# Cross-attention queries from split fp32r parts, the low parts kept over x, and a new order of the units around them

## The chip, the cores and the metric

One Trainium2 chip, one of its cores. The time is that of one execution on the device in microseconds (us). TensorE (PE), VectorE (DVE), ScalarE (ACT), GpSimd (POOL) and SyncE (SP, which here only starts DMAs) each run an instruction stream of their own, in order, and wait for each other through semaphores.

## The reference

A decoder layer over x and ctx of 8 batches x 512 rows x 256 columns, all fp32:

```python
x = layernorm(x + linear_attention(x))        # state memory, M=128, decay 0.99
x = layernorm(x + cross_attention(x, ctx))    # 16 heads of 16: q = x @ w_q.T + b_q; k, v from ctx
x = layernorm(x + self_attention(x) + moe(x)) # 16 heads; 8 experts 256x256, the two best by gate
```

The change is in `q = x @ w_q.T` of the cross attention, and in what lies around it.

## The kernel before

**Phases and slots.** Each batch n has a cross-attention phase C n and a self-attention phase S n. They run in the order C0, C1, S0, C2, S1, ..., C7, S6, S7. A phase has 16 slots, so slot s runs from 0 to 255, and each slot has two halves, an even and an odd one (t = 2s and 2s+1). In each half PE computes two score tiles `sc`, two tiles `mx` for the row maxima of a group six slots ahead, and in even halves also the product of probabilities and values `op`. ACT takes the exponential of `sc` (line 801), DVE the maxima of `mx` (line 990, three PSUM banks, one `mx` tile each).

**Units.** All other work of PE is cut into units: for a batch q1, k1, v1, s0, s1, s23, o1, y01, y23 (linear attention), x0 and x1 (transposes of the normalised rows x1 into x1T, 4 of 128x128 each), qc0 and qc1 (cross q), kc0, kc1, cv0, cv1 (cross k, v), hT, cy, x2T, k3c, q3c, v3, gate, be and moe0 to moe15, and for each group of four slots `shift` (a transpose of the maxima) and `heads` (4 transposes of oT). The tables LIN_* (relative to the start of phase C n), MID_* and MOE_* say in which half slot a unit stands. From slot 0 on, PE runs the units of both halves of a slot in its odd half, after `sc` and `mx`, in the order of the tables (line 725). For n of 3 to 7 the table LIN holds; phase C n starts at slot 32n-16.

**Banks.** Units write two PSUM banks `ms` in turn. A unit waits until the unit two before it has been taken out (lines 538 to 539):

```python
if u >= 2:
    wait_unit_out(pe, *ORDER[u - 2])
```

ACT and DVE take out the units of half t-1 when they come to half t. On ACT that is after its exponential of half t, on DVE after its two maxima of half t; a few kinds (EARLY_OUT) go ahead of the maxima, and only in even halves. So in a slot with `shift` (even half) DVE copies shift_r (line 954) behind the two maxima of the odd half.

**Cross q before.** Line 764 copies x0 and x1 on ACT into x1T (fp32); line 576 multiplies with the fp32 weight w_wq, two products of 512 columns in a unit. A product in fp32 stands in the trace as two instructions. The others of this kind (kc, cv, k3c, q3c, v3, moe) already use parts: a value is the sum of a high part rounded to fp32r (by ACT) and a low part, the rest (by DVE or POOL), and hi*hi + lo*hi + hi*lo is computed, six instructions in a unit (project_parts, line 502).

**Memory of x.** x_s holds x of a batch, then x plus the linear attention, and from n = 2 on also the staged context (load_ctx, ctx_high on ACT, ctx_low on POOL, line 1217). load_x brings the next batch's x, after ln_out[0] and ctx_low. x_bias (POOL, line 1213) adds a bias to it.

Of the kernel before, what the change touches and what calls it, by code (L numbers as in the profile page):

```python
# [12 lines left out]
P = 128  # L13
# [6 lines left out]
E = 8  # L20
# [28 lines left out]
             "x_bias": (-21, 0), "x1_bias": (-17, 0), "load_xT": (-21, 1), "load_x": (-12, 0)}  # L49
# [15 lines left out]
       "x_bias": (-27, 0), "x1_bias": (7, 0), "load_xT": (-31, 0), "load_x": (-11, 1), "load_ctx": (-17, 1),  # L65
# [17 lines left out]
MOE_FIRST = [(24, 1), (25, 1), (28, 0), (29, 1), (30, 1), (31, 0), (31, 1), (32, 1), (33, 0), (33, 1), (35, 1), (36, 1), (37, 0),  # L83
# [164 lines left out]
STAGED = ("we", "wqkv3", "be", "wk2", "wv2")  # L248
# [8 lines left out]
def decoder(nc, x, xT, ctxT, w, out):  # L257
    with ExitStack() as ctx:
        def sb(name, shape, dt=F32):
            return ctx.enter_context(nc.sbuf_tensor(name, shape, dt))  # L260
# [20 lines left out]
        combT = sb("combT", [TERMS * E, T])[:]  # L281
        gateT = sb("gateT", [P, P])[:]
# [3 lines left out]
        x2T_part = (sb("x2T_hi", [P, DC, T]), sb("x2T_lo", [P, DC, T]))  # L286
        part = {n: sb(n + "_parts", [P, 2, T]) for n in "qk"}
# [27 lines left out]
        comb3 = sb("comb3", [P, TB, TERMS * E])  # L315
# [35 lines left out]
        zeros, xb_out, x1b_out, x2_high, x2_low = sem("zeros"), sem("xb_out"), sem("x1b_out"), sem("x2_high"), sem("x2_low")  # L351
# [4 lines left out]
        LATE = tuple(n for n in w if n not in FIRST + EARLY + STAGED)  # L356
        block = ctx.enter_context(nc.Block())
# [33 lines left out]
        def _(sp):  # L391
            def load(name, n):
                if name == "load_xT":
                    if n >= 1:
                        wait_unit(sp, "k1", n - 1)
                        wait_unit(sp, "v1", n - 1)
                    sp.dma_start(xT_s[:], xT[n:n + 1].rearrange("o (c p) t -> p (o c) t", p=P)).then_inc(xT_in, 16)
                elif name == "load_x":
                    if n >= 1:
                        sp.wait_ge(ln_out[0], TB * n)  # L400
                    if n >= 3:
                        sp.wait_ge(ctx_low, DC * n)
# [75 lines left out]
        def _(pe):  # L478
# [23 lines left out]
            def project_parts(dst, wt, src, cols):  # L502

                for m, (i, j) in enumerate(((0, 0), (1, 0), (0, 1))):
                    for c in range(DC):
                        last = mm(dst, wt[j][:, c, cols].bitcast(F32R), src[i][:, c, :].bitcast(F32R),
                                  m == 0 and c == 0, m == 2 and c == DC - 1)
                return last

            def project_part_rows(bank, width, src, wt, cols, blocks):  # L510

                for b, t in enumerate(blocks):
                    for m, (i, j) in enumerate(((0, 0), (1, 0), (0, 1))):
                        for c in range(DC):
                            last = mm(bank[:, b * width:(b + 1) * width], src[i][:, c, t * P:(t + 1) * P].bitcast(F32R),
# [18 lines left out]
            def unit(task, n):  # L534
# [31 lines left out]
                elif task in ("kc0", "kc1"):  # L566
# [4 lines left out]
                    last = project_parts(bank, w2_part["wk2"], ctxT_part, slice(c * P, c * P + P))  # L571
                elif task in ("qc0", "qc1"):
# [3 lines left out]
                    last = project(bank, W["wq2"], x1T, slice(c * P, c * P + P))  # L576
                elif task in ("cv0", "cv1"):
# [4 lines left out]
                    last = project_part_rows(bank, D, ctxT_part, w2_part["wv2"], slice(0, D), (2 * h, 2 * h + 1))  # L582
# [19 lines left out]
                elif task in ("k3c0", "k3c1", "q3c0", "q3c1"):  # L602
# [6 lines left out]
                    last = project_parts(bank, w3_part, x2T_part, slice(at, at + P))  # L609
                elif task in ("v3a", "v3b"):  # L610
# [5 lines left out]
                    last = project_part_rows(bank, D, x2T_part, w3_part, slice(2 * D, 3 * D), (2 * h, 2 * h + 1))  # L616
# [116 lines left out]
        def _(act):  # L733
# [16 lines left out]
            def take_out(task, n):  # L750
# [92 lines left out]
            for t in range(FIRST_HALF, LAST_HALF + 1):  # L843
# [6 lines left out]
                if t == lin_at("y01", 0):  # L850
# [3 lines left out]
                    nc.scalar.mul(W["wq2"][:], W["wq2"][:], HD ** -0.5).then_inc(scaled, 1)  # L854
# [38 lines left out]
        def _(dve):  # L893
# [17 lines left out]
            def take_out(task, n):  # L911
# [55 lines left out]
                elif task in ("x2T0", "x2T1"):  # L967
                    c = int(task[3])
                    dve.wait_ge(x2_high, DC * n + c + 1)
                    nc.vector.tensor_tensor(x2T_part[1][:, c, :].bitcast(F32R), bank, x2T_part[0][:, c, :],  # L970
                                            ALU.subtract).then_inc(x2_low, 1)
# [211 lines left out]
        def _(pool):  # L1183
# [140 lines left out]
```

## Time and profile before

| | before |
|---|---|
| median of 3 runs | 1255.2 us (1250.92 to 1255.43) |
| profiled execution, its time | 1252.54 us |
| its span | 1250.8 us |
| busy PE, DVE, ACT, POOL | 96%, 74%, 62%, 31% |

The span reaches from the first to the last instruction; 1.7 us of the execution lie around it. Busy PE counts overlapping instructions once; a matmul's recorded duration is longer than the distance to the next one's start, so lengths in PE are read from start to start. Slot 0 starts at 67.69 us. Half slots are given below as stretches from one `sc` to the next.

### The profile page before, as it was taken

The page shows a single profiled execution, that of the slowest core. Times are in us where ns is not written, and L with a number is a line of the kernel's source. Part 1 is how long each engine was busy: PE and PEld are TensorE (multiplying, and loading weights), DVE is VectorE, ACT ScalarE, POOL GpSimd, SP SyncE. Part 2 cuts the span into 40 slices and gives each one's busy share as a digit, 9 for nine tenths or more (in the row PEclk, how much of TensorE's full clock was granted, in tenths as well). Part 3 has the DMA queues.
Part 4 walks back from the last instruction along what each step waited for, and adds up shares of the span by engine and source line. Part 5 has one row for each costly group of instructions (what it writes and reads, how often), then busy time and mean ns, then how long its engine had stood idle before and what let it go on. Part 6 is the DMA issues. An engine that isn't in the chain of part 4 may idle for free.

```text
span 1250.8 us, 20663 instructions
## 1 busy us (share of the span) xinstructions
PE 1204.7 (96%) x6998; PEld 599.3 (48%) x6998; DVE 922.8 (74%) x1867; ACT 778.6 (62%) x1090; POOL 381.9 (31%) x485
## 2 busy tenths in 40 slices
PE   8799999999999999999999999999999999999998
PEld 4443444545545445454554454454544444554443
DVE  3687886677777787777877778777877788678772
ACT  2355567675576665765667656667657666666664
POOL 5510113311522134420523206221153204430261
PEclk9999999999999999999999999999999999999999
DMA  7422122122222122222122222222122211212200
GB/s 251 118 57 65 44 52 69 44 52 57 56 69 63 36 66 57 61 65 54 48 63 70 56 56 69 47 66 52 40 57 68 52 39 42 67 28 52 52 19 18
DMA packets 56446, 74.99 MB, mean 60 GB/s; under 512 B 14720, under 2 KB 26520, under 8 KB 56088
## 3 DMA queue, kind: packets, MB, share of 16 engines
q1 hardware_dynamic: 55192, 72.96, 23.4%
q8 instruction: 57, 0.93, 0.3%
q10 hardware_dynamic: 1152, 0.72, 0.2%
q14 instruction: 45, 0.37, 0.1%
HBM read 18.06 MB, written 4.19 MB: 18 GB/s over the span
## 4 chain that ended last, share of the span: by engine, by line
PE 80%; DVE 7%; ACT 6%; issue 4%; SPq 1%; DMA 1%; ACTq 0%; POOL 0%; DVEq 0%
PE ms L480 36%; PE op L480 15%; PE sc L480 15%; PE mx L480 9%; DVE maxes L990 3%; ACT probs L801 3%; PE ms L590 2%; PE ms L531 2%; ACT moe L794 1%; SPq L427 1%; PE ms L585 1%; DMA w_ident<-in_ident 1%; ACT k_parts L737 1%; DVE q_parts L900 0%; DVE heads L963 0%
## 5 line engine op out<-in xcount | busy, mean ns | idle before, releaser
L990 DVE TENSOR_REDUCE maxes<-mx 128x1 f32<-128x512 f32 x1024 | 657.5, 684 | 198.7 <-PE mx L480 196.9
L801 ACT ACTIVATE probs<-sc 128x1024 f32<-128x1024 f32 x512 | 525.0, 1025 | 369.1 <-PE sc L480 364.9
L1240 POOL TENSOR_TENSOR x<-x,moe 128x256 f32<-128x256 f32 x256 | 187.4, 732 | 646.3 <-ACT moe L794 624.7
L480 PE MATMUL op<-probs,v 128*32 128x512 f32 x2048 | 272.8, 605 | 0.4 <-ACT probs L801 0.3
L480 PE MATMUL sc<-qs,ks 50*128 50x512 f32 x1024 | 256.3, 497 | 13.8 <-ACT probs L801 12.8
L480 PEld LDWEIGHTS sc<-qs,ks 50*128 50x128 f32 x1024 | 95.3, 183 | 307.1 <-ACT probs L801 234.8
L480 PE MATMUL mx<-ks,qs 48*128 48x512 f32 x1024 | 209.5, 404 | 8.9 <-DVE maxes L990 6.7
L794 ACT ACTIVATE moe<-ms,comb 128x256 f32<-128x256 f32 x256 | 107.1, 473 | 20.1 <-PE ms L480 20.1
L480 PEld LDWEIGHTS mx<-ks,qs 48*128 48x128 f32 x1024 | 97.4, 187 | 22.4 <-DVE maxes L990 16.6
L480 PE MATMUL ms<-we_hi,x2T_hi 128*128 128x512 f32 x256 | 92.8, 443 | 3.2 <-DVE q_parts L900 1.0
L480 PEld LDWEIGHTS op<-probs,v 128*32 128x32 f32 x2048 | 40.3, 108 | 93.7 <-issue 92.0
L480 PE MATMUL ms<-we_hi,x2T_lo 128*128 128x512 f32 x256 | 80.5, 395 | 0.0
L480 PE MATMUL ms<-we_lo,x2T_hi 128*128 128x512 f32 x256 | 80.4, 395 | 0.0
L480 PEld LDWEIGHTS ms<-we_hi,x2T_hi 128*128 128x128 f32 x256 | 39.4, 188 | 34.8 <-issue 14.7
L480 PEld LDWEIGHTS ms<-we_lo,x2T_hi 128*128 128x128 f32 x256 | 48.0, 188 | 11.8
L480 PEld LDWEIGHTS ms<-we_hi,x2T_lo 128*128 128x128 f32 x256 | 48.1, 188 | 11.7
L590 PE MATMUL ms<-w_ident,oT 128*128 128x128 f32 x256 | 41.0, 283 | 2.4 <-DVE shift_r L954 1.6
L900 DVE SCALAR_TENSOR_TENSOR k_parts<-ms,w_bk,k_parts 128x512 fp32r<-128x512 f32 x32 | 24.0, 751 | 25.2 <-ACT k_parts L737 24.2
L1195 POOL TENSOR_SCALAR var<-mv 128x4 f32<-128x4 f32 x24 | 5.5, 230 | 113.9 <-DVE mv L1021 98.8
L736 ACT ACTIVATE oT<-op 128x512 f32<-128x512 f32 x64 | 38.0, 594 | 1.4 <-PE op L480 1.4
L590 PEld LDWEIGHTS ms<-w_ident,oT 128*128 128x128 f32 x256 | 28.2, 141 | 21.9 <-DVE shift_r L954 16.7
L737 ACT ACTIVATE k_parts<-ms,w_bk 128x512 fp32r<-128x512 f32 x32 | 22.0, 686 | 24.5 <-PE ms L480 18.0
(155 smaller groups left out, 1302.4 us busy)
## 6 DMA issues: line engine op xcount, KB each, us to landing
ks<-k_parts SPq DMA_DIRECT2D x384, 64.0 KB, 2.3
qs<-q_parts SPq DMA_DIRECT2D x381, 64.0 KB, 2.2
xT_s<-in_xT SPq DMA_DIRECT2D x8, 512.0 KB, 3.8
x_s<-in_x SPq DMA_DIRECT2D x8, 512.0 KB, 4.2
out<-x SPq DMA_DIRECT2D x7, 512.0 KB, 3.1
x_s<-in_ctxT SPq DMA_DIRECT2D x6, 512.0 KB, 5.1
qs<-shift_r SPq DMA_DIRECT2D x128, 8.0 KB
x<-in_ctxT SPq DMA_DIRECT2D x2, 512.0 KB, 6.3
```

The lines of the kernel that those rows point to most:

```text
L427: sp.dma_start(dst[at:at + HD, g % RING, :, :], part[name][src:src + 32, which[r], :]).then_inc(stack_in[name][g % 2], 16)
L480: return nc.tensor.matmul(dst, lhsT, rhs, start=first, stop=last, skip_group_check=True)
L531: last = nc.tensor.transpose(bank[:, t * P:(t + 1) * P], src[:, t, c * P:(c + 1) * P], ident[:])
L585: last = nc.tensor.transpose(bank[0:SHIFT * HG * TB, 0:P], shift_n[:, n % 2].rearrange("p s a m -> p (s a m)"), ident[:])
L590: last = nc.tensor.transpose(bank[:, t * P:t * P + P], oT[:, t * P:t * P + P], ident[:])
L736: return nc.scalar.activation(dst, src, ACT.Copy)
L737: return nc.scalar.activation(dst, src, ACT.Identity, bias=bias, scale=1.0)
L794: nc.scalar.activation(moe[:, k % 2, j * D:j * D + D], bank[:, j * D:j * D + D], ACT.Copy, scale=comb[:, t, e:e + 1]).then_inc(moe_out, 1)
L801: nc.scalar.activation(probs[:, (2 * s + h) % 3, :, :], sc[:], ACT.Exp).then_inc(exp_out, 1)
L900: nc.vector.scalar_tensor_tensor(out=part[name][:, 1, :].bitcast(F32R), in0=unit_bank((task, n)), scalar=bias[:, c:c + 1], in1=part[name][ ...
L990: nc.vector.tensor_reduce(maxes[:, g % 2, at:at + 1], mx[:, i % 3, :], AX_X, ALU.max).then_inc(max_out, 1)
L1240: nc.gpsimd.tensor_tensor(x2[:, n % 2, t, :], x2[:, n % 2, t, :], moe[:, k % 2, j * D:j * D + D], ALU.add).then_inc(acc, 1)
```

## The change

Units qc0 and qc1 use parts of x1T and of wq2. The high parts lie where x1T lay, the low parts of x0 and x1 lie in the memory of x_s; DVE makes them. So x of the next batch can be loaded only after qc1, and load_x moves (LIN: from slot -11 to -4). x0 and x1 can be taken out only when the context staged in x_s has been split, and x0, x1 and qc0 move (LIN: from -16, -15, -14 to -14, -14, -13). In batch 2 s1, s23, o1, y01 and y23 move earlier, and in batch 0 one moe unit (35, 1) moves to (32, 0), with the next ones in turn. wq2 is staged over x2T_lo, scaled and rounded by ACT, and its low part made by POOL. combT, gateT and comb3 (the experts' weights, transposed) lie over o1T.

```diff
-             "x_bias": (-21, 0), "x1_bias": (-17, 0), "load_xT": (-21, 1), "load_x": (-12, 0)}
+             "x_bias": (-21, 0), "x1_bias": (-17, 0), "load_xT": (-21, 1), "load_x": (-5, 0)}
...
-              "x_bias": (-4, 0), "x1_bias": (20, 1), "load_xT": (-4, 0), "load_x": (3, 0), "load_ctx": (-13, 0),
+              "x_bias": (-4, 0), "x1_bias": (20, 1), "load_xT": (-4, 0), "load_x": (11, 0), "load_ctx": (-13, 0),
...
-LIN_THIRD = {"q1": (-37, 1), "k1": (-36, 1), "v1": (-41, 1), "s0": (-35, 1), "s1": (-34, 1), "s23": (-33, 1),
-             "o1": (-32, 1), "y01": (-30, 0), "y23": (-29, 0), "x0": (-20, 0), "x1": (-19, 0), "x_bias": (-34, 0),
+LIN_THIRD = {"q1": (-37, 1), "k1": (-36, 1), "v1": (-41, 1), "s0": (-35, 1), "s1": (-34, 0), "s23": (-34, 1),
+             "o1": (-33, 1), "y01": (-32, 0), "y23": (-32, 1), "x_bias": (-35, 0),
...
-       "o1": (-23, 1), "y01": (-21, 0), "y23": (-20, 0), "x0": (-16, 0), "x1": (-15, 0), "qc0": (-14, 0),
+       "o1": (-23, 1), "y01": (-21, 0), "y23": (-20, 0), "x0": (-14, 0), "x1": (-14, 1), "qc0": (-13, 0),
...
-       "x_bias": (-27, 0), "x1_bias": (7, 0), "load_xT": (-31, 0), "load_x": (-11, 1), "load_ctx": (-17, 1),
+       "x_bias": (-27, 0), "x1_bias": (7, 0), "load_xT": (-31, 0), "load_x": (-4, 0), "load_ctx": (-17, 1),
...
-MOE_FIRST = [(24, 1), (25, 1), (28, 0), (29, 1), (30, 1), (31, 0), (31, 1), (32, 1), (33, 0), (33, 1), (35, 1), (36, 1), (37, 0),
+MOE_FIRST = [(24, 1), (25, 1), (28, 0), (29, 1), (30, 1), (31, 0), (31, 1), (32, 0), (32, 1), (33, 0), (33, 1), (36, 1), (37, 0),
...
+        combT = over("combT", [TERMS * E, T], "o1T", 4 * T)[:]
+        gateT = over("gateT", [P, P], "o1T", 4 * T)[:]
+        comb3 = over("comb3", [P, TB, TERMS * E], "o1T", 4 * T)
+        x1T_part = ([over(f"x1T_hi{c}", [P, T], "x1T", 4 * T * (DC - c)) for c in range(DC)],
+                    [over(f"x1T_lo{c}", [P, T], "x_s", 4 * T * (DC - c)) for c in range(DC)])
+        wq2_part = (sb("wq2_hi", [P, DC, D]), sb("wq2_lo", [P, DC, D]))
...
                     if n >= 1:
-                        sp.wait_ge(ln_out[0], TB * n)
-                    if n >= 3:
-                        sp.wait_ge(ctx_low, DC * n)
+                        wait_unit(sp, "qc1", n - 1)
...
-                    last = project(bank, W["wq2"], x1T, slice(c * P, c * P + P))
+                    if n == 0:
+                        pe.wait_ge(wq2_low, 1)
+                    last = project_parts(bank, wq2_part, x1T_part, slice(c * P, c * P + P))
...
-                elif task in ("x0", "x1"):
-                    wait_unit(act, task, n)
-                    copy(x1T[:, int(task[1]), :], bank).then_inc(done, 1)
...
+                elif task in TRANSPOSED:
+                    name, c = task[:-1], int(task[-1])
+                    if name == "x2T" and n == 0:
+                        act.wait_ge(wq2_low, 1)
                     wait_unit(act, task, n)
-                    copy(x2T_part[0][:, int(task[3]), :].bitcast(F32R), bank).then_inc(x2_high, 1)
+                    copy(rows_part[name][0][c][:].bitcast(F32R), bank).then_inc(rows_high[name], 1)
...
+                elif task in TRANSPOSED:
+                    name, c = task[:-1], int(task[-1])
+                    dve.wait_ge(rows_high[name], DC * n + c + 1)
+                    if name == "x" and n >= 2:
+                        dve.wait_ge(ctx_low, DC * (n + 1))
+                    nc.vector.tensor_tensor(rows_part[name][1][c][:].bitcast(F32R), bank, rows_part[name][0][c][:],
+                                            ALU.subtract).then_inc(rows_low[name], 1)
...
-                    nc.scalar.mul(W["wq2"][:], W["wq2"][:], HD ** -0.5).then_inc(scaled, 1)
+                    act.wait_ge(wq2_in, 16)
+                    nc.scalar.mul(wq2_stage, wq2_stage, HD ** -0.5).then_inc(scaled, 1)
+                    act.wait_ge(scaled, 3)
+                    copy(wq2_part[0][:].bitcast(F32R), wq2_stage).then_inc(wq2_high, 1)
...
                     pool.wait_ge(w_late, 16 * len(LATE))
+                    pool.wait_ge(wq2_high, 1)
+                    nc.gpsimd.tensor_tensor(wq2_part[1][:].bitcast(F32R), wq2_stage, wq2_part[0][:], ALU.subtract).then_inc(wq2_low, 1)
```

A unit x0 or x1 now counts as out when DVE has written its low part (rows_low).

## Rows read from the trace of the kernel before

**Rows 1.** The page: busy time, share of the span and instructions of each engine.

```profile
PE 1204.7 (96%) x6998; PEld 599.3 (48%) x6998; DVE 922.8 (74%) x1867; ACT 778.6 (62%) x1090; POOL 381.9 (31%) x485
```

**Rows 2.** Windows: stretch, length, busy (count) per engine, granted clock, DMA share, GB/s.

```profile
355.53:357.80 2.27, 2.27 (x16) 1.35 (x12) 2.24 (x5) 1.56 (x3) 1.46 (x2) 1.00 0.26 58
372.56:375.21 2.65, 2.65 (x18) 1.73 (x14) 2.13 (x5) 2.65 (x6) 1.43 (x2) 1.00 0.18 34
376.88:379.91 3.03, 3.03 (x17) 1.52 (x13) 2.15 (x5) 1.81 (x4) 2.32 (x4) 1.00 0.00 0
381.58:383.82 2.24, 2.24 (x14) 1.42 (x11) 2.21 (x6) 1.03 (x1) 0.00 (x0) 1.00 0.32 73
230.39:234.04 3.65, 3.65 (x21) 2.55 (x17) 2.54 (x6) 1.03 (x1) 0.00 (x0) 1.00 0.39 88
417.73:420.90 3.17, 3.17 (x16) 1.39 (x12) 2.96 (x6) 1.51 (x2) 0.00 (x0) 1.00 0.36 83
```

**Rows 3.** Groups of instructions by line and shape: count, busy us, mean ns of one.

```profile
L970 DVE TENSOR_TENSOR x2T_lo<-ms,x2T_hi 128x512 fp32r<-128x512 f32 x16 | 10.9, 687 | 2.0 <-ACT x2T_hi L736 1.3
...
L736 ACT ACTIVATE x1T<-ms 128x512 f32<-128x512 f32 x16 | 9.6, 604 | 1.3 <-PE ms L531 1.3
```

**Rows 4.** Timeline of PE, odd half of slot 66: start, length, instruction.

```profile
377.54 0.28 PE L585 MATMUL ms<-w_ident,shift_n 128*32 128x128 f32 x1
377.66 1.89 PE L480 MATMUL ms<-x1T,w_wq 128*128 128x512 f32 x4
379.38 0.60 PE L590 MATMUL ms<-w_ident,oT 128*128 128x128 f32 x4
```

**Rows 5.** Timelines of DVE and ACT in the same half.

```profile
376.28 2.65 DVE L990 TENSOR_REDUCE maxes<-mx 128x1 f32<-128x512 f32 x4
378.85 0.27 DVE L954 COPY shift_r<-ms 32x128 f32<-32x128 f32 x1
...
377.42 1.02 ACT L801 ACTIVATE probs<-sc 128x1024 f32<-128x1024 f32 x1
```

**Rows 6.** Timeline of PE in slot 30, odd half: a unit behind shift's bank.

```profile
204.73 0.50 PE L480 MATMUL sc<-qs,ks 50*128 50x512 f32 x2
...
207.03 0.73 PE L480 MATMUL ms<-we_hi,x2T_hi 128*128 128x512 f32 x2 [0.91 <-DVE shift_r L954]
```

**Rows 7.** Timelines of PE and DVE in slot 75, odd half from 417.73.

```profile
418.99 1.99 PE L480 MATMUL ms<-x1T,w_wq 128*128 128x512 f32 x4
...
418.51 0.42 DVE L963 TENSOR_TENSOR heads<-ms,rsum 128x256 f32<-128x256 f32 x1
```

**Rows 8.** Windows: slots 28 and 29, then halves of slots 32, 14, 15, 16, 57.

```profile
194.69:203.07 8.38, 7.78 (x47) 4.37 (x43) 6.25 (x10) 6.24 (x10) 2.78 (x3) 1.00 0.49 125
216.07:218.70 2.63, 2.33 (x14) 1.34 (x10) 1.67 (x3) 2.63 (x6) 1.41 (x2) 1.00 0.23 54
126.68:129.75 3.07, 2.37 (x15) 1.11 (x12) 2.89 (x6) 1.02 (x1) 0.00 (x0) 1.00 0.01 3
131.41:133.03 1.62, 1.59 (x12) 0.97 (x8) 1.59 (x5) 1.02 (x1) 0.00 (x0) 1.00 0.35 81
134.71:138.17 3.46, 3.46 (x21) 2.12 (x18) 1.94 (x4) 1.51 (x2) 0.00 (x0) 1.00 0.41 95
336.70:339.71 3.01, 3.01 (x16) 1.73 (x12) 2.03 (x5) 1.56 (x3) 1.45 (x2) 1.00 0.36 121
```

**Rows 9.** The page's DMA issues; timelines of SP, POOL and DVE at the start.

```profile
x_s<-in_x SPq DMA_DIRECT2D x8, 512.0 KB, 4.2
...
47.34 3.75 SPq L427 DMA_DIRECT2D qs<-q_parts  x6
...
55.73 2.76 POOL L1213 TENSOR_TENSOR x_s<-x_s,w_bo 128x256 f32<-128x256 f32 x4
...
63.49 0.67 DVE L935 TENSOR_TENSOR x_s<-ms,x_s 128x512 f32<-128x512 f32 x1
```

**Rows 10.** Window at the start in which the granted clock was low.

```profile
46.00:48.00 2.00, 2.00 (x4) 0.71 (x3) 0.43 (x1) 0.00 (x0) 1.92 (x2) 0.50 0.60 98
```

More of the change, by code:

```diff
@@ L178 @@
 EARLY_OUT = ("s0", "s1", "s23", "v1", "y01", "y23", "cv0", "cv1", "cy0", "cy1", "v3a", "v3b", "shift", "gateT")
+TRANSPOSED = ("x0", "x1", "x2T0", "x2T1")
 SPLITS = ("kc0", "kc1", "qc0", "qc1", "k3c0", "k3c1", "q3c0", "q3c1")
 def own_signal(task):
-    return task in SPLITS or task in ("be0", "be1", "shift", "heads", "gateT", "x2T0", "x2T1") or task.startswith("moe")
+    return task in SPLITS or task in ("be0", "be1", "shift", "heads", "gateT") or task in TRANSPOSED or task.startswith("moe")
 TAKEN = {unit: sum(not own_signal(ORDER[v][0]) for v in range(u % 2, u + 1, 2)) for u, unit in enumerate(ORDER)}
@@ L247 @@
 EARLY = ("wv1", "bv1", "decay", "wo1", "bo1", "ident")
[L248 removed]
+STAGED = ("we", "wqkv3", "be", "wk2", "wv2", "wq2")
 def head_tile(i):
@@ L258, in decoder, with over @@
     with ExitStack() as ctx:
+        home = {}
         def sb(name, shape, dt=F32):
-            return ctx.enter_context(nc.sbuf_tensor(name, shape, dt))
+            tensor = ctx.enter_context(nc.sbuf_tensor(name, shape, dt))
+            home[name] = nc.sbuf_base
+            return tensor
+        def over(name, shape, other, end):
+            return nc.alloc_sbuf_tensor_at(name, shape, F32, offset=home[other] - end)
         def sem(name):
@@ L286, in decoder @@
         x2T_part = (sb("x2T_hi", [P, DC, T]), sb("x2T_lo", [P, DC, T]))
+        wq2_stage = over("wq2_raw", [P, DC, D], "x2T_lo", 4 * DC * T)[:]
+        ctx_chunks, x2T_chunks = ([[part[:, c, :] for c in range(DC)] for part in parts] for parts in (ctxT_part, x2T_part))
         part = {n: sb(n + "_parts", [P, 2, T]) for n in "qk"}
@@ L350, in decoder @@
         ln_out = [sem(f"ln_out{k}") for k in range(3)]
-        zeros, xb_out, x1b_out, x2_high, x2_low = sem("zeros"), sem("xb_out"), sem("x1b_out"), sem("x2_high"), sem("x2_low")
+        zeros, xb_out, x1b_out = sem("zeros"), sem("xb_out"), sem("x1b_out")
+        rows_high = {name: sem(name + "_high") for name in ("x", "x2T")}
+        rows_low = {name: sem(name + "_low") for name in ("x", "x2T")}
+        wq2_in, wq2_high, wq2_low = sem("wq2_in"), sem("wq2_high"), sem("wq2_low")
         g_step, g_exp = sem("g_step"), sem("g_exp")
@@ L570, in unit @@
                         pe.wait_ge(w2_low, 2)
-                    last = project_parts(bank, w2_part["wk2"], ctxT_part, slice(c * P, c * P + P))
+                    last = project_parts(bank, w2_part["wk2"], ctx_chunks, slice(c * P, c * P + P))
                 elif task in ("qc0", "qc1"):
@@ L581, in unit @@
                         pe.wait_ge(w2_low, 2)
-                    last = project_part_rows(bank, D, ctxT_part, w2_part["wv2"], slice(0, D), (2 * h, 2 * h + 1))
+                    last = project_part_rows(bank, D, ctx_chunks, w2_part["wv2"], slice(0, D), (2 * h, 2 * h + 1))
                 elif task == "shift":
@@ L608, in unit @@
                     at = (D if task[0] == "k" else 0) + c * P
-                    last = project_parts(bank, w3_part, x2T_part, slice(at, at + P))
+                    last = project_parts(bank, w3_part, x2T_chunks, slice(at, at + P))
                 elif task in ("v3a", "v3b"):
@@ L615, in unit @@
                         pe.wait_ge(w3_cut, 4)
-                    last = project_part_rows(bank, D, x2T_part, w3_part, slice(2 * D, 3 * D), (2 * h, 2 * h + 1))
+                    last = project_part_rows(bank, D, x2T_chunks, w3_part, slice(2 * D, 3 * D), (2 * h, 2 * h + 1))
                 elif task == "gate":
@@ L966, in take_out @@
                                             ALU.mult).then_inc(heads_out, 1)
[L967 to L971, printed above, removed]
+                elif task in TRANSPOSED:
+                    name, c = task[:-1], int(task[-1])
[4 more added lines that the diff above has]
+                                            ALU.subtract).then_inc(rows_low[name], 1)
                 elif task == "gateT":
```

15 lines of the change are left out of this document (6 added, 9 removed).

## The prediction

> **What bounds the kernel now.** I read the page first: PE is busy 96% of the span, DVE 74%, ACT 62% [rows 1]. So the question of any edit is what it does to PE's stream. A share alone doesn't say whether PE works or waits its turn inside a slot, so I next cut the span into half slots, from one `sc` to the next, and read each as a window [rows 2]. The odd half of slot 61 holds sc, mx and one moe unit and takes 2.27 us; that of slot 65 holds x1 as well, four transposes, and takes 2.65: four transposes cost 0.38, one 0.1. Slot 67 with kc0 alone takes 2.24, slot 35 with a moe unit and kc0 3.65: a second unit of six part products costs 1.4. sc and mx take the first 0.66 of a half (376.88 to 377.54) [rows 2, 4], so a parts unit that comes first takes 2.24 - 0.66 = 1.58.
>
> The third view, the timelines of three engines in slot 66, shows what matters here. The half starts at 376.88. DVE is through its maxima at 378.93, and only then copies shift_r, until 379.12: 2.24 after the start [rows 5]. PE did qc0 meanwhile, 377.66 to 379.38, so nobody waited: `heads`, which has the bank of `shift`, could begin at 379.38 [rows 4]. Slot 30 shows the case without such a cover: PE stood idle for 0.91, and the unit behind shift's bank began at 207.03, 2.30 after its half (204.73), with shift_r named as the releaser [rows 6]. **A unit that needs shift's bank does not start before 2.30.**
>
> **Part 1: the units themselves.** qc0 in fp32, four instructions, takes 1.72 in slot 66 [rows 4]. In slot 75, qc1 waits for DVE to take `heads` out (ends 418.93), begins at 418.99 and ends the half 1.91 later, at 420.90 [rows 2, 7]. With parts I put 1.58 there, the same wait before it: 3.17 becomes 2.83, -0.34 in each of batches 2 to 7. In batch 1 both units stand between `shift` and `heads` as in slot 66; the half can fall only to the bound, 2.30 + 0.53 for four transposes (379.38 to 379.91) = 2.83 instead of 3.03: -0.2 twice, **-0.4**.
>
> **Part 2: the new order in batches 3 to 7.** All in odd halves:
> Slots 64 and 65 lose the transposes, 2.65 to 2.27: -0.38 twice, -0.76.
> Slot 66 was shift, qc0, heads; now shift, x0, x1, heads. x1 has shift's bank: start at 2.30. `heads` has x0's bank, and x0 is out only after its low part. ACT's exponential ends at 378.44, 1.56 after the start [rows 5], its copy of x0 takes 0.60 [rows 3]: about 2.1. DVE is free at 2.24 and needs 0.69 for a low part (x2T_lo is the same operation) [rows 3]: about 2.9. Heads start at 2.91, end the half 0.53 later, 3.44 against 3.03: +0.41.
> Slot 67 was kc0 alone, 2.24; now qc0, kc0. Without a wait it would be 3.65. But qc0 needs x1's low part. x1 stands in the odd half, so ACT copies it in the next even half behind the exponential (about 2.1 from that half's start), and DVE's low part behind that ends at 2.8; PE sees it at 2.85. By the same clock qc0 could have started at 1.66 (length of an even half, from 379.91 on) + 0.66 = 2.32. Wait 0.53, the half 4.18: +1.94.
> Slots 64 to 67: -0.76 + 0.41 + 1.94 = +1.59; with qc1 +1.25 for a batch, **+6.3 for five**. PE's work hardly changes; a unit of 1.7 that covered DVE's lateness is moved away, and short transposes with a slow way out stand there instead. The bounds: no wait at all, rival 2; every wait 0.1 to 0.2 longer (ACT's or DVE's start behind a semaphore), +8.
>
> **Part 3: batch 2.** Late part: slots 28 and 29 (8.38, PE idle 0.60 of it) lose x0 and x1 and the idle time with them: -0.76 - 0.60 = -1.36. Slot 32 gets a second moe unit, 2.63 to 3.65: +1.02. Slot 33 keeps two. Slot 34 as slot 66: +0.41. Slot 35 from 3.65 to 4.18: +0.53. With qc1's -0.34: +0.26 [rows 2, 8]. Early part: slot 14 (3.07, PE busy only 2.37 of it) gets s23 behind shift's bank, some 0.6 that nothing covers: +0.6. Slot 15 had s23 alone and took 1.62; it gets o1, which alone takes 3.01 in slot 57: +1.39. Slot 16 changes o1 (3.46 with heads) for y01 and y23, whose eight short products weigh the same: 0 to -0.1. Slots 18 and 19 lose y01 and y23, some 1.7 of PE work; there PE waits for the normalisation on DVE, so I take -0.2. Together +1.7; the bounds are +0.2, if all 1.7 come back, and +2.0 [rows 8]. **Batch 2: +2.0.**
>
> **Part 4: the start, and what costs nothing.** One copy more on ACT (0.6) and one subtraction on POOL stand where these engines idle. In batch 0 the low parts of x0 and x1 delay qc0 by 0.7, and SP, which has the k stacks to issue first, takes its result later than that: 0 to 0.7, I take +0.1. load_x of batch 1 stood ahead of six stacks issued from 47.34 to 51.1; it goes behind them. Landing takes 4.2 in the median, so 55.3. POOL begins x_bias at 55.73 and needs 2.76, DVE reads it at 63.49 [rows 9]: covered by 5. Without the cover, a landing after 60.7, it costs what it is late, up to 3. In later batches it lands eight slots before x_bias. SP waits at load_x for qc1, and behind it stands only stack_q, which needs qc1 too; the shifts' DMAs come two slots later. DVE's wait for ctx_low stands behind POOL's work of the slot before: no wait; were it late, it would show as idle DVE in slot 66. The 16 low parts are 11 us of new work on an engine busy 923 of 1251; the wait for those in slots 66 and 67 is priced, the others lie in DVE's idle time. The buffers put over o1T wait for nothing new: 0.
>
> **The clock.** It was granted in full, 1.00, in slots 28 and 29, with 0.60 of idle time and eight transposes [rows 8]; at the start it once read 0.50, 1.2 GHz [rows 10]. The Trainium skill, "TensorE: Matmul & The Clock Gate", Part 4: PE-mode transpose, says that transposes don't count as busy for the clock in the way that matmuls do. By that the new slot 66, 13 transposes and over 1 us of idle time, could bring the clock down, and the sum would be rival 6's. The trace of slots 28 and 29 speaks against it. The sum goes by the rows.
>
> **Sum.** 6.3 + 2.0 - 0.4 + 0.1 = +8.0. The span goes from 1250.8 to 1258.8, this execution from 1252.54 to 1260.5. The median of the runs shown is 2.7 above this execution; scaled by 1258.8/1250.8 it is 1263.2. **I predict 1263 us.**
>
> **Rivals.** Times are on the scale of the median.
> 1. The forecast, in full or for the most part: +4 to +11, 1259 to 1266. Chance 0.60 (0.46 beyond 0.5%, 0.14 short of it).
> 2. The waits are hidden and only PE's work counts. For it: PE is 96% busy. Against it: the idle time in slot 30. Slot 66 would take 0.66 + 0.12 (shift) + 1.2 (12 transposes) + 0.2 = 2.2 and slot 67 3.65; slots 64 to 67 change by -0.76 - 0.83 + 1.41 = -0.2, with qc1 -0.5 for a batch, -2.6 over five; batch 1 gives -0.4, batch 2 about +1: -2, 1253. It decides if DVE comes to shift_r 1 us sooner than in the rows. This is the case that is not slower. 0.18 (0.15 within 0.5%, 0.03 faster).
> 3. Each of the 16 units saves 0.34 and the new order costs nothing, since the lighter slots 64 and 65 let the engines behind run ahead: -5.5, 1249.7 or less. Against it: the gap behind shift_r doesn't depend on the slots before. 0.07, faster.
> 4. DVE becomes the bound: the 12 low parts in batches 2 to 7 lie on the path in full, 12 x 0.69 = +8 on top, 1271. Against it: in slot 67's long half DVE can catch up. 0.08.
> 5. x of batch 1 comes late, up to +3 on top: 1266. 0.05.
> 6. The clock falls in slots 66 and 67 of six batches; the 2.8 us of qc0 and kc0 take twice as long, +17 on top: 1280. 0.02.
>
> **Numbers.** 0.5% is about what a measurement of this kernel can tell from no change: 1248.9 to 1261.5. Slower 0.46 + 0.08 + 0.05 + 0.02 = 0.61; same 0.14 + 0.15 = 0.29; faster 0.10. The range for 8 in 10 takes in rivals 1, 2 and 5 and reaches to rival 4's near side: 1252 to 1270. The forecast's own is 1259 to 1266.
>
> **What would show it.** In the profile after: slot 66's odd half near 3.4, x1's transposes 2.30 after its start behind shift_r and heads behind x0's low part; slot 67's near 4.2, with PE idle 0.5 before qc0 until DVE's low part; slots 64 and 65 at 2.27, slot 75 at 2.83, slot 15 near 3.0. I am wrong if slot 66 stays at 3.0 or less, if qc0 starts without a gap, or if slots 16 to 19 give back what the y units weigh.

## The result, and the profile after

The changed kernel took 1270.1 us (median of four executions, 1266.67 to 1273.44), the kernel before beside it 1253.3: a ratio of 1.0141, 95% interval 1.0118 to 1.0165. The forecast was 1263, the range ended at 1270. A second set of executions of the same kernel gave 1267.05 (e0 below). So slower, as forecast, by more than forecast: +16.8 us between the medians and +14.1 between the two profiled spans (1250.8 and 1264.9), where the sum said +8.0. The two longest of the four executions, 1273.12 and 1273.44, had a mean granted clock of 0.987, the other two 0.991 and 0.993.

The page of the changed kernel, busy time and share of the span of each engine, then the granted clock in 40 slices:

```profile
PE 1209.0 (96%) x7030; PEld 608.7 (48%) x7030; DVE 934.5 (74%) x1883; ACT 779.8 (62%) x1091; POOL 384.3 (30%) x486
...
PEclk9989999999999999999999999999999999999899
```

Against [rows 1], PE's busy time grew by 4.3 us and DVE's by 11.7. Neither is 14, and no share moved by more than one point: the page alone doesn't find the loss.

Windows of the changed kernel (columns as in [rows 2]): the odd halves of slots 64, 65, 66, 67 and 75, then slots 28 (odd half) and 29, then the odd halves of slots 14 and 15:

```profile
371.14:373.41 2.27, 2.27 (x15) 1.35 (x11) 1.69 (x3) 2.06 (x4) 1.48 (x2) 1.00 0.77 178
375.07:377.95 2.88, 2.34 (x14) 1.35 (x10) 2.35 (x5) 2.70 (x5) 1.40 (x2) 1.00 0.31 62
379.61:383.09 3.48, 2.57 (x22) 1.67 (x19) 2.77 (x6) 2.06 (x4) 2.34 (x4) 1.00 0.00 0
384.75:388.95 4.20, 3.68 (x22) 2.48 (x18) 3.35 (x7) 2.11 (x3) 0.00 (x0) 1.00 0.00 0
422.80:425.67 2.87, 2.87 (x18) 1.76 (x14) 2.84 (x7) 1.51 (x2) 0.00 (x0) 1.00 0.39 90
198.24:205.10 6.86, 6.67 (x38) 3.45 (x34) 5.40 (x10) 5.27 (x8) 1.95 (x3) 1.00 0.44 95
127.75:131.52 3.77, 3.07 (x20) 1.75 (x16) 3.22 (x7) 1.02 (x1) 0.00 (x0) 1.00 0.01 3
133.18:136.20 3.02, 3.02 (x16) 1.74 (x12) 2.18 (x5) 1.02 (x1) 0.00 (x0) 1.00 0.42 99
```

Read them against [rows 2, 8]. Slot 64 fell from 2.65 to 2.27, slot 66 rose from 3.03 to 3.48 (forecast 3.44), slot 67 from 2.24 to 4.20 (4.18), slot 75 fell from 3.17 to 2.87 (2.83), slot 14 rose from 3.07 to 3.77 and slot 15 from 1.62 to 3.02. All of that stood in the prediction. Slot 65 is the odd one: forecast 2.27, here 2.88, and 2.64 in the later batches. It lost four transposes and gained nothing.

The two waits stand where they were forecast. Timeline of PE in slots 66 and 67 of the changed kernel (start, length, instruction, idle time before it and its releaser):

```profile
379.61 0.50 PE L497 MATMUL sc<-qs,ks 50*128 50x512 f32 x2
...
381.90 0.66 PE L548 MATMUL ms<-w_ident,x 128*128 128x128 f32 x4 [0.91 <-DVE shift_r L976]
382.50 0.66 PE L609 MATMUL ms<-w_ident,oT 128*128 128x128 f32 x4
...
384.75 0.50 PE L497 MATMUL sc<-qs,ks 50*128 50x512 f32 x2
385.09 0.40 PE L497 MATMUL mx<-ks,qs 48*128 48x512 f32 x2
386.01 0.69 PE L497 MATMUL ms<-x1T_hi,wq_hi 128*128 128x512 f32 x2 [0.52 <-DVE x1T_lo L994]
```

x1 begins 2.29 after its half, behind shift_r (forecast 2.30); qc0 waits 0.52 for the low part (0.53).

Slot 65 needs two engines. PE's timeline of the changed kernel at the end of that half:

```profile
376.78 0.63 PE L497 MATMUL ms<-we_lo,x2T_hi 128*128 128x512 f32 x2
377.95 0.50 PE L497 MATMUL sc<-qs,ks 50*128 50x512 f32 x2 [0.55 <-ACT probs L820]
```

and ACT's over the same half:

```profile
374.87 0.83 ACT L813 ACTIVATE moe<-ms,comb 128x256 f32<-128x256 f32 x2
375.84 1.16 ACT L755 ACTIVATE ctxT_hi<-x_s 128x512 fp32r<-128x512 f32 x2
376.90 1.00 ACT L820 ACTIVATE probs<-sc 128x1024 f32<-128x1024 f32 x1
```

ACT takes out the moe unit, then makes both high parts of ctx (1.16), and only then the exponential that the next `sc` needs. PE stands for 0.55 at the end of the half. Before, x1's transposes filled just that time. The row for it was in the prediction: [rows 2] give ACT 2.65 busy of slot 65's 2.65.

Where the 14.1 us went, from the starts of the slots in the two traces (each row is rounded):

| stretch | forecast | found |
|---|---|---|
| slots 64 to 67 and their like, batches 3 to 7 | +7.95 | +10.1 |
| the rest of those batches (slot 75 and its like) | -1.7 | -1.7 |
| batch 2, without the clock (slots 14 to 63) | +2.0 | +0.6 |
| slot 19, clock at one half | 0 | +1.2 |
| batch 1 (slots 6 and 10) | -0.4 | 0.0 |
| start to the end of slot 2 | +0.1 | +1.2 |
| slots 237 to 240, clock at one half | 0 | +3.0 |
| elsewhere | 0 | -0.2 |

The split of batch 2 from the clock rests on e4, e8 and e10: slots 17 to 19 took 19.9 to 20.0 us there at full clock, 20.56 in the kernel before and 21.14 after.

Two windows of the changed kernel show what the clock rows look like; the number before the DMA share is the granted clock, 0.50 being 1.2 GHz of 2.4:

```profile
71.00:78.00 7.00, 6.31 (x24) 2.44 (x25) 4.50 (x13) 4.50 (x7) 1.72 (x4) 0.50 0.06 13
...
1185.50:1192.30 6.80, 6.80 (x23) 3.03 (x22) 3.17 (x6) 2.05 (x2) 0.61 (x1) 0.50 0.33 78
```

### The profile page after: what moved, and what is told of

Read it like the earlier page. It is cut to its first block, busy times and chain, and to the rows that moved or that the text cites. A ratio compares the mean times of both kernels' runs of the same rounds, so it can differ in the third digit from the quotient of the medians.

```text
span 1264.9 us, 20757 instructions
## 1 busy us (share of the span) xinstructions
PE 1209.0 (96%) x7030; PEld 608.7 (48%) x7030; DVE 934.5 (74%) x1883; ACT 779.8 (62%) x1091; POOL 384.3 (30%) x486
## 4 chain that ended last, share of the span: by engine, by line
PE 78%; DVE 8%; ACT 7%; issue 4%; SPq 1%; DMA 1%; ACTq 0%; DVEq 0%
PE ms L497 35%; PE op L497 15%; PE sc L497 15%; PE mx L497 8%; DVE maxes L1014 4%; ACT probs L820 4%; PE ms L609 2%; PE ms L548 2%; SPq L443 1%; ACT moe L813 1%; PE ms L604 1%; ACT k_parts L756 0%; DVE q_parts L922 0%; DVE heads L985 0%; ACT q_parts L756 0%
## 5 line engine op out<-in xcount | busy, mean ns | idle before, releaser
L497 PE MATMUL op<-probs,v 128*32 128x512 f32 x2048 | 275.7, 610 | 0.4 <-ACT probs L820 0.3
L813 ACT ACTIVATE moe<-ms,comb 128x256 f32<-128x256 f32 x256 | 107.1, 473 | 19.9 <-PE ms L497 19.7
L1237 POOL TENSOR_TENSOR x_s<-x_s,w_bo 128x256 f32<-128x256 f32 x32 | 22.4, 730 | 45.0 <-DMA x_s<-in_x 44.9
```

Of the source, the lines that this page charges most:

```text
L497: return nc.tensor.matmul(dst, lhsT, rhs, start=first, stop=last, skip_group_check=True)
L813: nc.scalar.activation(moe[:, k % 2, j * D:j * D + D], bank[:, j * D:j * D + D], ACT.Copy, scale=comb[:, t, e:e + 1]).then_inc(moe_out, 1)
L1237: nc.gpsimd.tensor_tensor(x_s[:, t, :], x_s[:, t, :], W["bo1"][:], ALU.add).then_inc(xb_out, 1)
```

## The experiments

The theory: the order of units around `shift` costs what the prediction says, and the rest is the clock and slot 65. The rivals: the 16 low parts load DVE (rival 4), or the parts cost something by themselves. Ratios are against executions of the kernel before on the same chip. "LIN" is the table of batches 3 to 7.

**e0, the changed kernel again.**

> The changed kernel once more, unchanged. What I now hold: of the 14.1 us that its profiled span is longer, some 8.7 come from the half slots of batches 3 to 7 (slot 67 +1.95, slot 66 +0.45, slot 64 -0.39, slot 65 0, slot 75 -0.32 each) and some 5 from stretches at the lower clock level: 23.9 us at clock 0.50 in three places after slot 0 and one before it, against 6.8 us in the kernel before. Theory A (the low stretches belong to the new order of units): the profile shows them again at the same three places, near 69 to 80, 155 to 158 and 1185 to 1192 us, and the time is 1267 to 1273. Theory B (they fall by chance in light stretches): another profile has them elsewhere or not at all, the half slots of batches 3 to 7 unchanged, and times scatter by some 6 us with the mean clock of the run.

1267.05 us (1264.64 to 1268.31), ratio 1.0124 (1.0095 to 1.0153), span 1262.7. Same halves as above, but for slot 65's, which took 3.02 here and 3.11 in batch 4 (e7 says why); slots 237 to 240 took 16.35 here, against 16.36 before and 19.32 in the first profile. So those 3.0 us are not a property of the kernel.

**e1, the order alone.** The kernel before, fp32 q, with three places changed:

```diff
-"x0": (-16, 0), "x1": (-15, 0), "qc0": (-14, 0),
+"x0": (-14, 0), "x1": (-14, 1), "qc0": (-13, 0),
```

> The kernel before, fp32 cross q as it was, with only x0, x1 and qc0 of batches 3 to 7 moved to slots -14, -14 and -13. Theory of the cover (moving qc0 away from between shift and heads costs the time): slot 66's odd half 3.03 to about 3.3 (x1 waits for shift's bank until 2.30, heads for ACT's copy of x0 only), slot 67's 2.24 to about 4.06 (0.66 + 1.8 for qc0 in fp32 + 1.6 for kc0, no wait), slot 64 -0.39, slot 65 0: +1.7 per batch, +8.5 us in all, 1262 us. Rival (the low parts on DVE make the loss): the order alone costs less than 3 us, 1256 or less.

1262.38 us, ratio 1.0084 (1.0057 to 1.0111). Slots 64 to 67 took 18.83 instead of 17.24: +1.6 a batch, without any parts. The halves of slots 66 and 67, windows of e1:

```profile
377.14:380.46 3.32, 2.41 (x21) 1.66 (x18) 2.15 (x5) 2.05 (x4) 2.32 (x4) 1.00 0.00 0
382.11:386.07 3.96, 3.96 (x19) 2.11 (x16) 2.64 (x6) 2.12 (x3) 0.00 (x0) 1.00 0.00 0
```

In slot 66 PE is idle for 0.91 of 3.32. The order is the main cause; with the parts slot 66 is 0.15 longer and slot 67 0.24. Slot 65 stayed at 2.64, without a part of x in it, and PE waits 0.30 for ACT's exponential at its end: its floor is ACT's.

**e2, the parts alone.** The changed kernel with batches 3 to 7 at the old places; their low parts lie in o1T and lin:

```diff
-"x0": (-14, 0), "x1": (-14, 1), "qc0": (-13, 0),
+"x0": (-16, 0), "x1": (-15, 0), "qc0": (-14, 0),
...
+late_low = [over("x1T_late0", [P, T], "o1T", ...), over("x1T_late1", [P, T], "lin", ...)]
```

> The changed kernel with x0, x1 and qc0 of batches 3 to 7 back at slots -16, -15 and -14, which is possible because their low parts lie over o1T and over a free part of lin instead of over x_s. Theory of the cover: slot 66's odd half 2.83 to 2.89 (bound by shift_r at 2.30 and heads), slot 67's 2.24, slots 64 and 65 2.66, slot 75 2.85: -2.1 us per batch against the changed kernel, -10.5 in all, 1259 to 1260 us. Rival (the parts and their low parts on DVE cost by themselves, wherever they stand): it stays within 3 us of the changed kernel, 1267 or more.

1256.13 us, ratio 1.0037 (1.0021 to 1.0053): 11 below e0 with the same low parts on DVE, and 3 below what was expected. Slots 64 to 67: 17.60, slot 67 2.25, slot 75 2.85. DVE's load is not the main cause. But 17.60 is still above 17.24, since slot 66 took 3.39; e6 takes that up.

**e3, batch 2's early units back.** The changed kernel with s1, s23, o1, y01, y23 of batch 2 where they were before.

> The changed kernel with s1, s23, o1, y01 and y23 of batch 2 back where they stood. Slots 14 to 19 took 33.70 us before and 36.22 after. If the order of these units costs it: -1.5 to -2.5 us, with slot 15 at 1.62, slot 18 near 2.55 and slot 19 near 5.0. If the 2.2 us in slot 19's even half is the lower clock and nothing else, about 0.3 us comes back from the order and the rest depends on whether the clock falls there again; then -0.3 to -2.5 us without a clear verdict in the median, and slot 19's even half is 3.65 where the clock reads 1.00.

1262.32 us, ratio 1.0091 (1.0061 to 1.0122): 4.7 below e0, where 2.5 at most was expected. Slots 14 to 16 fell from 15.08 to 13.15, slots 17 to 19 were 20.61, and the stretch of low clock in slot 19 was gone.

**e4 and e10, slot 18 filled.** The changed kernel with two fp32 products of 256 columns more in slot 18's odd half, which the change empties:

```diff
+if s == 18:
+    u = PLACE["x2T0", 0]
+    wait_unit_out(pe, *ORDER[u - 2])
+    busy(2, D, ms[:, u % 2, :])
```

> The changed kernel, with two fp32 products of 256 columns, 0.86 us of TensorE work that nothing uses, in slot 18's odd half, where y01 of batch 2 stood before. In all three profiles in which y01 and y23 had left slots 18 and 19 the granted clock was 0.50 for 3.4 us just behind slot 18; in the three in which they stood there it was not. Theory (the lighter slot 18 lets the clock fall): the low stretch near 154 us is gone, slots 17 to 19 take 20.6 us instead of 21.1 to 21.5, and the mean clock of the runs rises from 0.990 by some 0.003; the time falls by 1 to 3 us although work was added. Rival (chance): the low stretch stays, or comes as often as before, and the time doesn't fall.

> The changed kernel with two fp32 products of 256 columns added in slot 18's odd half, once more. If filling that half keeps the clock up: no half-clock stretch within 145 to 160 us and slots 17 to 20 at 19.9 to 20.6 us. If the first look was chance: a stretch of 3.4 us or more there and 21.1 us or more. Time 1262 to 1266 us by either, since what is at stake is 1.2 us.

e4 1265.42 us, ratio 1.0101 (1.0069 to 1.0132); e10 1263.33, ratio 1.0103 (1.0086 to 1.012). No half clock near 154 us in either, slots 17 to 19 at 19.94 and 19.95. The half grew by 0.86 and slot 19 gave it back (8.53 against 9.35 in e8, both at full clock): the work is free. The ten executions of e4 and e10 had a mean granted clock of 0.988 to 0.999, 0.995 on average; the nine of the changed kernel 0.987 to 0.993, 0.991 on average. In time, e4 lies within the noise of e0, and e10 is 3.7 below it.

**e5 and e6, the old orders, then ctx's low part later.** e5 is e2 with e3's table; only x0, x1 and qc0 of batch 2 keep their new places. e6 moves one operation of POOL in batches 3 to 7:

```diff
-"ctx_high": (-15, 0), "ctx_low": (-15, 0)}
+"ctx_high": (-15, 0), "ctx_low": (-14, 1)}
```

> Parts for cross q with the low parts of batches 3 to 7 over o1T and lin, x0, x1 and qc0 of these batches where they stood before, and s1, s23, o1, y01 and y23 of batch 2 where they stood before: the arithmetic of the change with almost the order of before. By the sum of the bands of slots in the profiles: batches 3 to 7 +0.35 in slots 64 to 67 and -0.33 in slot 75, so 0; batch 2 -0.4, so 1251 to 1253 us, within 0.2% of the kernel before. If the two orders are all that the change costs, this is no slower than before; if the parts themselves cost, it is 1255 or more. A gain over 3 us is expected by nobody: the parts save TensorE time in halves that DVE bounds.

> As e5, with POOL's ctx_low of batches 2 to 7 one slot and a half later, behind the addition of moe10. In every batch one shift_n instruction of DVE (16 elements a partition, 0.18 us elsewhere) takes 1.2 us exactly while POOL's ctxT_lo runs, and both end together. Theory (the two contend): these shift_n fall to 0.18, x1's low part comes 1 us sooner, slot 66's odd half falls from 3.39 to 2.85: some -0.4 per batch, -2 us in all against e5, 1249 to 1251 us. Rival (the long shift_n has another cause): it stays at 1.2 us there; or it moves to whatever stands beside ctxT_lo now, and nothing is gained.

e5 1254.46 us, ratio 1.0026 (1.0011 to 1.004), slot 66 3.39: between the two outcomes named for it. e6 1250.61 us, ratio 0.9986 (0.9974 to 0.9999), slot 66 2.88. Timeline of DVE in e5, ahead of slot 66's odd half (376.13):

```profile
374.40 1.21 DVE L1028 SCALAR_TENSOR_TENSOR shift_n<-maxes,shift_n 128x16 fp32r<-128x16 f32 x1
375.53 0.68 DVE L998 TENSOR_TENSOR x1T_late<-ms,x1T_hi 128x512 fp32r<-128x512 f32 x1
376.13 2.56 DVE L1018 TENSOR_REDUCE maxes<-mx 128x1 f32<-128x512 f32 x4
```

The timeline of POOL in e5 over the same time:

```profile
373.04 2.54 POOL L1245 TENSOR_TENSOR ctxT_lo<-x_s,ctxT_hi 128x512 fp32r<-128x512 f32 x2 [3.59 <-ACT ctxT_hi L759]
```

The timeline of DVE in e6, where that half starts at 377.58:

```profile
375.65 0.17 DVE L1028 SCALAR_TENSOR_TENSOR shift_n<-maxes,shift_n 128x16 fp32r<-128x16 f32 x1
376.37 0.69 DVE L998 TENSOR_TENSOR x1T_late<-ms,x1T_hi 128x512 fp32r<-128x512 f32 x1 [0.54 <-ACT x1T_hi L759]
```

The same operation on 16 columns takes 0.17 alone and 1.21 beside POOL's, and both end together (375.61 and 375.58). In e5 the second low part of x1 so starts only 0.60 before the half, in e6 1.21; DVE enters the half's maxima late in e5, PE's `mx` waits 0.23 for it, and shift_r and what needs its bank come late in turn. So a low part of 0.68 on DVE just ahead of the maxima does cost a little, though DVE's load as a whole doesn't.

**e7, more work for PE in the wait.** The changed kernel with one fp32 product of 512 columns between x0 and x1 in slot 66 (batches 3 to 7):

```diff
+if task == "x1" and n >= 3:
+    i = 4 * (start_of("C", n) - 14 + MAX_LEAD) + 2
+    pe.wait_ge(max_out, i)
+    busy(1, T, mx[:, (i + 2) % 3, :])
```

> The changed kernel with one fp32 product of 512 columns, 0.85 us of TensorE work that nothing uses, between x0 and x1 in slot 66 of batches 3 to 7, in the mx bank that is free then. Theory of the cover (PE is idle there, waiting for shift_r): it costs nothing, slot 66's odd half stays at 3.48 and the time at that of the changed kernel, 1266 to 1270. Rival (PE's work sets the slot): +0.85 in each of five batches, +4.3 us, slot 66 at 4.3.

1266.57 us, ratio 1.0113 (1.009 to 1.0136), level with e0. PE's timeline of e7 in that half:

```profile
383.15 0.50 PE L497 MATMUL sc<-qs,ks 50*128 50x512 f32 x2
...
384.38 1.02 PE L497 MATMUL mx<-w_decay,w_ident 128*128 128x512 f32 x2
385.46 0.66 PE L548 MATMUL ms<-w_ident,x 128*128 128x128 f32 x4
```

The added product lies in the wait, x1 still begins 2.31 after its half, and the half takes 3.49 instead of 3.48. Five times 0.85 of work cost nothing: the half is bound by shift_r, not by PE. Slot 65 took 3.87 in that profile, for another reason. ACT's timeline of e7 there:

```profile
379.38 1.15 ACT L759 ACTIVATE ctxT_hi<-x_s 128x512 fp32r<-128x512 f32 x2 [1.13 <-DMA x_s<-in_ctxT]
```

PE's timeline of e7 at the end of that half:

```profile
381.49 0.50 PE L497 MATMUL sc<-qs,ks 50*128 50x512 f32 x2 [1.54 <-ACT probs L824]
```

The staged ctx landed late, and the half grew with ACT's wait for it. In the trace of before no such copy in slots past the start waited for the DMA; in the changed kernel one did (0.13), in e0 two (0.28 and 0.36), in e7 two (1.13 and 0.64), in e3, e10 and e15 one each (0.73, 0.86, 0.98), always in batches 3 and 4. The halves with these waits took 2.88, 3.02, 3.11, 3.87, 3.38, 3.48, 3.60 and 3.72: each is its wait plus 2.74 or 2.75. That shows without a new edit that ACT sets the length of slot 65. With the old order of batches 3 to 7 two of ten profiles had such a wait (e6 0.45, e12 0.40), with the new one six of eight.

**e8, batch 2's early order alone.** The kernel before with s1, s23, o1, y01 and y23 of batch 2 at the change's places, and no more; e12, e13 and e14 are three more profiles of it.

```diff
-"s1": (-34, 1), "s23": (-33, 1), "o1": (-32, 1), "y01": (-30, 0), "y23": (-29, 0),
+"s1": (-34, 0), "s23": (-34, 1), "o1": (-33, 1), "y01": (-32, 0), "y23": (-32, 1),
```

> The kernel before, with only s1, s23, o1, y01 and y23 of batch 2 put where the change has them (order of work alone, no arithmetic changed). Theory (the emptied half of slot 18 is what makes TensorE's clock fall near 154 us): a stretch of half clock of 3.4 us or more near 150 to 156 us, as in all four profiles with that order and in none of the six without it; slots 14 to 17 take 15.1 us instead of 13.15; time 1254 to 1258 us. Rival (those four were chance, or need the new parts in the other batches too): no such stretch, slots 17 to 20 at most 20.6 us, time 1253 to 1254.5.

> The kernel before with only the order of batch 2's y01 and y23 and what goes before them changed, a second profile. If the order alone brings the clock down after slot 18: in at least one of three such profiles a half-clock stretch between 148 and 158 us, with slots 17 to 20 at 21.1 us or more. If the new parts are needed too: none, slots 17 to 20 at 19.9 us each time.

> The same kernel, a third profile: the same two outcomes; the span is 1252 to 1254 us without a stretch at 148 to 158 us, and 1.2 us more or above with one.

> The same kernel, a fourth profile: a stretch at 148 to 158 us, if the order alone brings it, or none, if the parts are needed too.

e8: 1257.18 us (1255.72 to 1261.78), ratio 1.0055 (1.0037 to 1.0072), as the theory expected. But its profile had full clock in slots 17 to 19 (19.91), against the theory. The three further ones (1260.08, 1258.17 and 1256.01 us, beside 1251.72 of the kernel before) had half clock for 10.2 us from 151.4 to 151.8, and 23.24, 23.34 and 23.53 for slots 17 to 19. Windows of e12 over slot 18's odd half and slot 19:

```profile
148.50:150.19 1.69, 1.15 (x9) 0.47 (x5) 1.55 (x6) 1.02 (x1) 1.10 (x2) 1.00 0.00 0
150.19:162.87 12.68, 10.64 (x38) 6.01 (x37) 7.00 (x13) 4.42 (x6) 3.46 (x7) 0.60 0.00 1
```

Windows of e10 over the same two:

```profile
148.88:151.43 2.55, 2.01 (x15) 1.07 (x11) 2.25 (x9) 1.02 (x1) 1.77 (x4) 1.00 0.00 0
151.43:159.96 8.53, 6.63 (x37) 3.85 (x37) 6.00 (x11) 4.20 (x6) 2.79 (x4) 1.00 0.01 4
```

Slot 19 takes 12.68 with the clock down and 8.53 without, nearly the same instructions in it. The profile that kept its clock, e8's, over the same two:

```profile
149.33:151.01 1.68, 1.14 (x11) 0.46 (x7) 1.55 (x6) 1.03 (x1) 1.11 (x2) 1.00 0.00 0
151.01:160.36 9.35, 6.66 (x37) 3.86 (x37) 6.70 (x13) 4.21 (x6) 3.46 (x7) 1.00 0.01 2
```

The filled half also shortens the wait that opens slot 19, since DVE is late there in any case. PE's timeline of e12 (in e10 the same wait is 0.72):

```profile
152.27 0.80 PE L480 MATMUL mx<-ks,qs 48*128 48x512 f32 x2 [1.57 <-DVE maxes L990]
```

Whether the thin half or the longer wait behind it lets the clock fall, no run tells apart. Over all 18 profiles: of nine whose slot 18 was emptied, eight had half clock (3.4 to 10.2 us) there; of nine in which it was filled or in the old order, none.

**e9 and e11, who gets e6's gain.** e9 is the kernel before with e6's one move, e11 is e6 again.

> The kernel before, with only GpSimd's low part of ctx issued one unit later (ctx_low at -14,1 in place of -15,0, batches 3 to 7). Theory (in the kernel with parts and the old order, that half slot was long only because DVE's rows that end on the parts were stretched by GpSimd's op, and the kernel before has no such rows on its path): slots 64 to 68 stay at 17.24 us within 0.1 and the time within 0.1% of the kernel before. Rival (the overlap costs the kernel before too): slot 66's odd half falls from 3.03 to about 2.9 or less, and the time by 1 us or more.

> The kernel with parts, the old order and the later low part of ctx, once more, beside the kernel before with that one move. If the parts themselves pay (slot 75's half 3.175 to 2.85 in six batches, slots 28 to 31 shorter by 1.5 us): 1250 to 1251.5 us and 1 to 3 us below the run beside it. If the move of ctx's low part is what paid: the two within 1 us of each other.

e9 1251.95 us, ratio 1.0006 (0.9993 to 1.002), slots 64 to 67 at 17.27 as before: the move does nothing there. That nothing late stands behind the stretched operation is the likely reason. e11 1250.88 us, ratio 1.0005 (0.9988 to 1.0023), 1.1 below e9, on the line between the two outcomes. e6 and e11 together are level with the kernel before to 1 us or so: parts in the old order lose nothing, and no gain is settled.

**e15, the changed kernel, a third profile.**

> The changed kernel, a third profile. If the stretch after slot 18 belongs to its order: half clock for 3.4 us near 154 us again, slots 17 to 20 at 21.1 us or more. If the stretch of 10.2 us in slots 1 to 3 and the one near slot 239 are chance from run to run: at least one of them is missing here.

1264.28 us, span 1262.3. Half clock from 150.7 for 10.2 us and slots 17 to 19 at 23.19; slots 237 to 240 at 16.34. The stretch in slots 1 and 2 came again (6.8 us), but slot 0 had begun at 64.40 and slot 2 ended at 77.55, against 78.52 in the kernel before. It also stood in e1, whose program there is the kernel before's. Slot 2 ended at 76.6 to 84.1 in the eleven profiles with the change's start and at 74.4 to 78.9 in the seven with the old one: whether the new start costs 1 or 2 us stays open.

## Why the prediction was right in direction and short in size

Two steps of the sum failed, and both made it short: slot 65's -0.38, which measured 0 (part 2), and the clock, put at 0, which fell behind slot 18 (below). The waits at slots 66 and 67, most of the +8.0, came as forecast. The first set's median lies just outside the range, the second set's, 1267.05, inside it.

**What bounds the kernel, and the bound of 2.30 behind shift_r.** Right, shown by slot 66 in the changed kernel, by e1 without parts, and by e7, where PE got 0.85 more to do at no cost. Rival 2 (the waits are hidden) falls with it.

**Part 1, the units.** Slot 75: -0.34 forecast, -0.3 found, in e2 and e6 too. Batch 1 failed in the small: slot 10 fell by 0.16, slot 6 rose by 0.14. There x1's low part (0.68 on DVE) stands right ahead of the half's maxima, and PE's `mx` comes 0.52 after `sc` instead of 0.33, as in e5.

**Part 2, slots 64 to 67.** Slots 64, 66 and 67 came within 0.04. **The term that failed is slot 65's -0.38.** I took a transposing unit's price from slot 61, where ACT has 1.56 to do, and used it in slot 65, where ACT was busy for the whole half. What lies beside a full engine can't be taken out of the path. Five times 0.38 is 1.9 of the 2.1 missing; most of the rest is ctx landing late in batch 3. Rival 4 (DVE the bound, +8) is ruled out by e2, rival 3 (the new order costs nothing) by e1.

**Part 3, batch 2.** Slots 14, 15, 28, 29, 32, 34 and 35 within 0.2 each. Two terms were too dear: slots 17 to 19 give back 0.65, not 0.2 (e8, e10), and slot 36 gives back 0.75, where the moe unit no longer waits 0.71 for a k part, most likely since the slot before is longer. So +0.6 for +2.0. With slot 16's 0.2, slots 16 to 19 gave back 0.8 of the 1.7 that the y units weigh; the prediction had named that as a sign of being wrong, and it came half true. Slot 65's error and this one partly cancel, which is luck: the new order and the parts together cost +9.0 at full clock, for +8.0.

**Part 4 and rival 5.** Covered as forecast: the late x cost no wait that shows on PE's path. It didn't come eight slots ahead in batch 2, though: x_bias waited for it and began at 118.50, 21 us before DVE reads its result.

**The clock. This was the term left out.** It was weighed for slots 66 and 67 only (rival 6), and there it stayed at 1.00 in every profile, as slots 28 and 29 had shown. It fell in slot 19, at half clock for 3.4 us in the first profile and 10.2 in the third, which cost 1.2 to 3.2 us. In the sum slots 18 and 19 "lose some 1.7 of PE work" and that was booked as a small gain. The changed kernel's three profiles against e4 and e10 show that work in slot 18 holds the clock, and e8 that without it the fall is likely, not certain. The Trainium skill, "TensorE: Matmul & The Clock Gate", Part 1, says that the gate goes by how busy the engine has been of late. By that e10 should keep its clock more easily than e12, with 2.01 against 1.15 us of busy PE in slot 18's odd half, and so it was; e8 kept it at 1.14. The Trainium skill's rule on transposes (the same page, Part 4: PE-mode transpose), weighed in the prediction, is neither shown nor refuted: slot 19 holds eight transposes, and in e10 they ran at full clock.

Whole executions bear this out. At an equal mean granted clock of 0.992 two executions of the changed kernel took 1264.28 and 1266.84 us and six of the kernel before 1255.55 to 1256.04: 8.2 to 11.3 apart, around the +9.0 of order and parts. The medians of the first set are 16.8 apart, with clocks of 0.987 to 0.993 against 0.992 to 0.999 in all executions of the kernel before that stood beside the experiments. And e3 was 4.7 us below e0, of which the order explains 1.3. The 3.0 us in slots 237 to 240 differ from one execution to the next: ten of 18 profiles have half clock there, in kernels of every kind. The 1.2 at the start is not settled (e15).

**What stays open.** Why one profile of nine (e8's) kept its clock with slot 18 emptied, at the same 1.14 us of busy PE there. Whether the unprofiled executions lost their clock in the same place: their mean granted clock, 0.987 to 0.993 for the changed kernel and 0.989 to 0.996 for e8, fits it, and so do the 0.995 on average of e4 and e10 and the 0.995 to 0.997 of e3; but it has no place in time. And why two executions of the first set fell as low as 0.987.

## What to carry to other kernels

Price the removal of work from a slot by the fullest engine in that slot, not by the same work elsewhere: the window row lists all five. An engine's work that fills another's lateness is worth its place: before moving a long unit off a wait, ask what will stand in it. And when an edit empties a stretch in which PE already waits, give the clock a term of its own, and read it in more than one profile, since the same kernel kept its clock once and lost it three times (e8, e12 to e14).

## What the runs showed of the hardware

A small DVE operation with two SBUF inputs waited out a GpSimd operation that reads SBUF: shift_n<-maxes,shift_n, 0.17 us alone, took 1.20 to 1.21 in each of batches 3 to 7 of both kernels, ending with ctxT_lo. Where ctxT_lo was moved away (e6 and e9) it fell to 0.17 or 0.18 in all five. The Trainium skill, "SBUF — State Buffer", section "Who interferes with whom", says that a DVE instruction with two SBUF inputs contends with a GpSimd instruction that reads SBUF, and that the port pair which the two share is an exclusive lock; 1.21 against 0.17 agrees. It costs nothing in the kernel before (e9) and 0.5 a batch where a low part stands behind it (e5 against e6).

The load of ctx, 512 KB, has little to spare. In batches 5 to 7 its reader on ACT comes 6.0 to 6.1 us after the issue in the kernel before and 5.7 in the changed kernel, since slot 64 got 0.4 shorter. In batch 3 it was issued at 370.29 in the changed kernel and its reader began at 375.84, 5.55 later, 0.13 of it a wait; in the kernel before the reader came 5.64 after the issue and didn't wait. In e7 it took 6.5. So a load turned into a wait in six of eight profiles with the new order, where the slots ahead of its reader are shorter, and in two of ten with the old one.
